# Graph network with two layers on one core: layer 0's bias moved from a matmul to GpSimd, and two comparisons joined

## The reference, cut to what matters

```
h = relu(layernorm(x))
deg = segment_sum(ones, src); feat = h * clip(deg, 1)**-0.5
s = relu(segment_sum(feat[src], dst))
x = x + (s @ W.T + b)                       # layer 0
h = relu(layernorm(x))
m = segment_sum(h[src] @ W_msg.T + b_msg + edge_embed[type], dst)
x = x + gru(m, h, W_ih, W_hh, b_ih, b_hh)   # layer 1
```

## Time and profile before

| | before |
|---|---|
| median of 3 executions | 918.85 us (918.78 to 919.85) |
| the profiled execution | 920.79 us, of which the span is 918.8 us |
| granted TensorE clock over the span | 0.984 |
| TensorE, VectorE, ScalarE, GpSimd busy | 845.8, 772.6, 502.3, 96.9 us |

### The profile page before, as it was taken

How to read it: one execution, slowest core, us unless ns; L and a number is a source line. 1 busy time by engine, 2 the same in 40 slices (tenths; PEclk the granted TensorE clock), 3 DMA queues, 4 the chain that set the end, 5 groups by cost and what they waited for, 6 DMA issues and landing times.

```text
span 918.8 us, 21032 instructions
## 1 busy us (share of the span) xinstructions
PE 845.8 (92%) x8962; PEld 755.5 (82%) x8962; DVE 772.6 (84%) x1044; ACT 502.3 (55%) x924; POOL 96.9 (11%) x77
## 2 busy tenths in 40 slices
PE   2353899999999999999999999999999999999996
PEld 2242788889888888988889988989889888988985
DVE  5898999999999999999999991568766766766876
ACT  1579588888888888888888884211111111111011
POOL 6880203003020030100000000000000000000000
PEclk9995899999999999999999999999999999999998
DMA  3642434336444344543335510497667667667750
GB/s 89 136 142 74 166 145 168 153 151 236 195 179 167 152 172 195 211 181 147 152 146 212 211 34 13 156 299 267 236 272 283 226 248 299 236 233 290 260 211 20
DMA packets 38332, 169.17 MB, mean 184 GB/s; under 512 B 8132, under 2 KB 21387, under 8 KB 35288
## 3 DMA queue, kind: packets, MB, share of 16 engines
q1 hardware_dynamic: 31898, 159.98, 46.2%
q0 software_dynamic: 6000, 6.48, 2.9%
q10 hardware_dynamic: 334, 1.29, 0.5%
HBM read 87.67 MB, written 79.74 MB: 182 GB/s over the span
## 4 chain that ended last, share of the span: by engine, by line
PE 52%; DVE 31%; issue 6%; ACT 5%; POOL 4%; DMA 1%; SPq 0%; DVEq 0%; POOLq 0%; ACTq 0%
PE ps L1323 29%; DVE work L743 11%; DVE work L736 11%; PE ps L1182 9%; PE ps L1171 5%; DVE work L751 4%; POOL tab L494 3%; ACT ring L976 2%; ACT tab L987 1%; PE ps L1275 1%; PE ps L1278 1%; PE ps L1280 1%; PE ps L1276 1%; PE ps L1277 1%; PE ps L1279 1%
## 5 line engine op out<-in xcount | busy, mean ns | idle before, releaser
L1171 PE MATMUL ps<-work 128*128 128x106 f16 x3125 | 431.3, 216 | 46.7 <-ACT ring L976 29.0
L1182 PE MATMUL ps<-ring,tab 125*128 125x250 f16 x2500 | 417.2, 272 | 0.7 <-ACT ring L981 0.7
L976 ACT ACTIVATE ring<-ps 128x848 f16<-128x848 f32 x375 | 330.6, 884 | 75.3 <-PE ps L1171 68.8
L1171 PEld LDWEIGHTS ps<-work 128*128 128x128 f16 x3125 | 286.5, 101 | 70.5 <-ACT ring L976 33.2
L1323 PE MATMUL ps<-ring,tab 125*128 125x250 f16 (+1 forms) x2500 | 277.0, 269 | 0.0
L1323 PEld LDWEIGHTS ps<-ring,tab 125*128 125x128 f16 (+1 forms) x2500 | 242.4, 97 | 28.7
L1182 PEld LDWEIGHTS ps<-ring,tab 125*128 125x128 f16 x2500 | 244.5, 98 | 25.3 <-ACT ring L981 0.9
L736 DVE TENSOR_TENSOR work<-iota_row,mch 128x3906 f16<-128x3906 f16 x100 | 223.4, 2234 | 1.0 <-PE ps L1171 0.5
L743 DVE TENSOR_TENSOR work<-iota_w,mch 128x1550 f16<-128x1550 f16 x200 | 188.1, 981 | 0.0
L824 DVE TENSOR_TENSOR work<-work,ring 125x3250 f16<-125x3250 f16 (+1 forms) x92 | 161.6, 1780 | 0.0
L1119 ACT ACTIVATE tab<-ps,bg 128x250 f32<-128x250 f32 x25 | 11.8, 471 | 147.7 <-PE ps L1276 146.9
(11 more groups left out here) (187 smaller groups left out, 617.3 us busy)
## 6 DMA issues: line engine op xcount, KB each, us to landing
adjacency<-ring SPq DMA_DIRECT2D x23, 2937.5 KB
ring<-adjacency SPq DMA_DIRECT2D x46, 812.5 KB, 6.4
ring<-adjacency SPq DMA_DIRECT2D x46, 750.0 KB, 9.0
adjacency<-ring SPq DMA_DIRECT2D x23, 183.1 KB
out<-x_sb SPq DMA_DIRECT2D x24, 125.0 KB
h_turned<-hst SPq DMA_DIRECT2D x23, 125.0 KB, 2.0
tab<-h_turned SPq DMA_DIRECT2D x23, 125.0 KB, 2.0
x_sb<-x SPq DMA_DIRECT2D x3, 560.0 KB
```

What stands on the lines that cost most here:

```text
L976: act.activation(to(x * 2 * u, 2, x), ps[:, s:s + 2, 0:x * SLOTS].rearrange("p b (x h) -> p h b x", h=SLOTS), ACT.Copy).then_inc(sem("evac ...
L1171: last = pe.matmul(ps[:, 2 * (u % 2) + i // BANKW, o:o + WCOLS], lohot[:, s, k, :], combo[:, s, k, :], start=True, stop=True)
L1182: mm = pe.matmul(psD[c % 2], tabv[0][P, h, s, :], adj[c % 2][P, h, :], start=i == 0, stop=i == 2 * BLOCKS - 1)
```

## The change

It has three parts. `split_bias`, its tiles and the bias matmul leave; `psX` holds the product alone. GpSimd adds the bias to x itself, both nodes of a chunk in one instruction of 256 elements, 25 of them; they stand in its queue behind the gather of chunk 11 and a wait for the finished table (`tab0`), since the table is made of x without the bias, and ahead of the gather of chunk 12. `post0_x_vector` waits for its chunk's addition (`biased`). And in `onehots` one comparison covers the columns of both nodes, where two did.

```
--- before.py
+++ after.py
@@ -69,7 +69,7 @@
 
 SEMAPHORES = """
 heads_in weights_in dst_in x_in0 x_in1 x_in2 x_in3 x_in4 ends_set ends_in
-iotas consts consts0 headhots hist totals counted rows_i bias_parts later_in cand_in0 cand_in1 cand_in2 cand_in3 cand_in4 cand_in5 run_i
+iotas consts consts0 headhots hist totals counted rows_i biased later_in cand_in0 cand_in1 cand_in2 cand_in3 cand_in4 cand_in5 run_i
 runs_in0 runs_in1 runs_in2 runs_in3 runs_in4 runs_in5
 squares sq_sum wm_norm gsc_set scaled g_col emb_in odd0 odd1 a_square a_root scale0 h0 rows_v tab0_hi tab0
 fields lo_keys turned mch_keys mch onehot built spent evac adj_out0 adj_out1 types_moved
@@ -183,8 +183,6 @@
         ones = sb("ones", [128, 128], F32)
         onesh = sb("onesh", [128, 1], F16)
         iota_s = sb("iota_s", [128, CHUNKS + 1], F16)
-        onesb = sb("onesb", [128, LO], BF16)
-        b_parts = sb("b_parts", [128, CB, D], BF16)
         thr = sb("thr", [128, CHUNKS], F32)
         thr_odd = sb("thr_odd", [128, CHUNKS], F32)
         thr_key = sb("thr_key", [128, CHUNKS], F32)
@@ -249,8 +247,6 @@
         sq, at = carve(early, at, 3, D)
 
         embf = temps[0:TYPES, :].bitcast(F32)[:, 0:D]
-        bias_high, at = carve(early, at, D)
-        bias_rest, at = carve(early, at, D)
         cand, at = carve(early.bitcast(I32), at, CHUNKS, CAND)
         signs, at = carve(early, at, JUNK * CAND // 2)
         signs = signs.bitcast(F16).rearrange("p (k n) -> p k n", k=JUNK)
@@ -476,9 +472,7 @@
             gp.tensor_scalar(ident3[:, :], ident[:, :], float(TB), None, ALU.mult)
             gp.tensor_scalar(nident3[:, :], ident[:, :], -float(TB), None, ALU.mult)
             gp.iota(beyond[:, :], [[WIN, AHEAD]], base=KEY + WIN, channel_multiplier=0, allow_small_or_imprecise_dtypes=True)
-            gp.memset(onesb[:, :], 1.0)
             gp.memset(least[:, :], 2e-35)
-            gp.memset(b_parts[:, :, :], 0.0)
             gp.iota(thr_key[:, :], [[WIN, CHUNKS]], base=-KEY, channel_multiplier=BLOCKS,
                     allow_small_or_imprecise_dtypes=True)
             gp.iota(iota_row[:, :], [[1, LO + 1]], base=KEY, channel_multiplier=0, allow_small_or_imprecise_dtypes=True)
@@ -509,7 +503,16 @@
             run_edges(2)
             for m in (3, 4, 5):
                 candidates(m)
-            for g in range(3, CHUNKS):
+            for g in range(3, 3 + RAW):
+                run_edges(g)
+            for g in range(3 + RAW, 6 + RAW):
+                run_edges(g)
+
+            gp.wait_ge(sem("tab0"), TBATCHES)
+            for k in range(CHUNKS):
+                gp.tensor_tensor(x_sb[P, blocks(k), :], x_sb[P, blocks(k), :],
+                                 b0_sb[P, :].unsqueeze(1).broadcast_to([LO, CB, D]), ALU.add).then_inc(sem("biased"), 1)
+            for g in range(6 + RAW, CHUNKS):
                 run_edges(g)
 
 
@@ -599,7 +602,6 @@
             v.memset(epst[:, :], EPS)
             search_heads(v, ch)
             weight_squares(v, ch)
-            split_bias(v, ch)
             v.wait_ge(sem("consts"), 1)
             search_runs(v, ch, 0)
             row_stats(v, ch, 0, 0, XB)
@@ -607,23 +609,6 @@
             row_stats(v, ch, 1, 0, XB)
             unpack(v, ch, 0, 1)
             scale_weights(v, ch)
-
-        def split_bias(v, ch):
-
-            ch.did(v.tensor_copy(b_parts[0:1, 0, :], b0_sb[0:1, :]))
-            ch.did(v.tensor_copy(bias_high.bitcast(BF16)[:, 0:D], b0_sb[:, :]))
-            ch.wait()
-            ch.did(v.tensor_copy(b_parts[0:1, 1, :], b_parts[0:1, 0, :]))
-            ch.did(v.tensor_tensor(bias_rest, b0_sb[:, :], bias_high.bitcast(BF16)[:, 0:D], ALU.subtract))
-            ch.wait()
-            ch.did(v.tensor_copy(bias_high.bitcast(BF16)[:, D:2 * D], bias_rest))
-            ch.wait()
-            ch.did(v.tensor_tensor(bias_rest, bias_rest, bias_high.bitcast(BF16)[:, D:2 * D], ALU.subtract))
-            ch.did(v.tensor_copy(b_parts[32:33, :, :], bias_high.bitcast(BF16)[32:33, D:2 * D].unsqueeze(1)
-                                 .broadcast_to([1, CB, D])))
-            ch.wait()
-            v.tensor_copy(b_parts[64:65, :, :], bias_rest[64:65, :].unsqueeze(1).broadcast_to([1, CB, D]))\
-             .then_inc(sem("bias_parts"), 1)
 
         def weight_squares(v, ch):
 
@@ -738,14 +723,12 @@
                 iota_row[:, 0:even].rearrange("p (n t) -> p n t", t=2).unsqueeze(1)
                     .broadcast_to([128, n, even // 2, 2]),
                 lo2.unsqueeze(2).broadcast_to([128, n, even // 2, 2]), ALU.is_equal))
-            for d in range(WIN):
-                cols = slice(SLOTS * d, SLOTS * d + BLOCKS)
-                ch.did(v.tensor_tensor(
-                    combo[:, s, 0:n, cols].rearrange("p k (a t) -> p k a t", t=2),
-                    iota_w[:, cols].rearrange("p (n t) -> p n t", t=2).unsqueeze(1)
-                        .broadcast_to([128, n, BLOCKS // 2, 2]),
-                    col2.unsqueeze(2).broadcast_to([128, n, BLOCKS // 2, 2]), ALU.is_equal))
-            ch.wait(but=WIN)
+            blocks_of = lambda a: a.rearrange("p k (d h) -> p k d h", d=WIN)[:, :, :, 0:BLOCKS]
+
+            ch.did(v.tensor_tensor(blocks_of(combo[:, s, 0:n, :]),
+                                   blocks_of(iota_w[:, :].unsqueeze(1).broadcast_to([128, n, WCOLS])),
+                                   col2.unsqueeze(2).broadcast_to([128, n, BLOCKS, 2]), ALU.is_equal))
+            ch.wait(but=1)
             if b == 0:
                 v.wait_ge(sem("mch"), c + 1)
             v.tensor_tensor(typehot[:, s, 0:n, :, :],
@@ -755,6 +738,7 @@
 
         def post0_x_vector(v, ch, k):
 
+            v.wait_ge(sem("biased"), k + 1)
             v.wait_ge(sem("psX"), k + 1)
             v.tensor_tensor(x_sb[P, blocks(k), :], psX, x_sb[P, blocks(k), :], ALU.add).then_inc(sem("x1"), 1)
             v.wait_ge(sem("x1"), k + 1)
@@ -1189,12 +1173,9 @@
             positive(pe, sem("tab_lo"), k)
             if k == 0:
                 pe.wait_ge(sem("later_in"), 16)
-                pe.wait_ge(sem("bias_parts"), 1)
             for j in range(CB):
-                pe.matmul(psX[:, j, :], aggr[:, LO * j:LO * (j + 1)], w0_sb[:, :], start=j == 0, stop=False,
-                          skip_group_check=True)
-            pe.matmul(psX, onesb[0:65, :], b_parts[0:65, :, :], start=False, stop=True, skip_group_check=True)\
-              .then_inc(sem("psX"), 1)
+                last = pe.matmul(psX[:, j, :], aggr[:, LO * j:LO * (j + 1)], w0_sb[:, :], start=True, stop=True)
+            last.then_inc(sem("psX"), 1)
 
         def post0_turn_tensor(pe, k):
             pe.wait_ge(sem("h1"), k + 1)
```

22 lines of the change are left out of this document (1 added, 21 removed).

## The result

| | before | after |
|---|---|---|
| median of 5 executions | 918.85 us (918.78 to 919.85) | 924.21 us (923.82 to 924.46) |
| the profiled execution, its span | 920.79, 918.8 us | 924.46, 922.7 us |
| granted TensorE clock over the span | 0.984 | 0.975 |

The changed kernel is slower by 5.4 us: the ratio to before is 1.0053, with a 95% interval of 1.0042 to 1.0064. The forecast was 922.8 us with a range of 914 to 930, and slower as its likeliest side.

A forecast was written before the change was run, and what follows sets the result against it. VectorE and TensorE were taken as a nearly level pair, VectorE slower by 0.56 us per three chunks. The terms -1.4 - 2.8 - 2.4 + 10.5 gave +3.9 us on 918.85, so 922.8 us, range 914.0 to 930.0.

The forecast's parts named there:

- The additions: GpSimd's 25 additions, in chunks 2 to 4: each costs VectorE 0.46 us by its SBUF reads, 11.5 us together.
- The lower bound of 0.08 us: VectorE's loss per addition if the addition's length does not matter: 2.0 us for all 25.
- the upper one of 0.77 us: VectorE's loss per addition if GpSimd keeps it out for reads and writes, 768 elements: 19.2 us for all 25.
- The joined comparison: VectorE's two comparisons of 1550 elements become one of 3100: 0.08 us saved per batch, 0.32 per chunk.
- The rival of a slow form: The joined comparison falls to one element per cycle, 150 us more, some 1070 us; chance 0.03.
- The start: GpSimd's gathers up to 60 us: without its two memsets and VectorE's bias split, -1.4 us, from -0.4 to -2.
- The stalls: TensorE's five 0.56 us stalls in chunks 5 to 17 go as both engines stand level: -2.8 us.
- The lower bound, -1 where VectorE still trails: The smaller gain from TensorE's stalls in chunks 5 to 17 if VectorE still trails: -1 us.
- The matmul: The bias matmul leaves TensorE's path, 0.11 us per chunk over 20 chunks and 2 at the tail: -2.4 us.
- The rule weighed in the prediction: Second to issue at SBUF blocks fully until the first finishes: additions would cost 14 us, the whole change +6.4.

The follow-up runs named there:

- wide_adds: The changed kernel with the bias sum made in five GpSimd instructions (one of 256 elements, four of 1536) instead of 25: 927.16 us, ratio 1.0085.
- sets: The changed kernel with each addition replaced by a memset of 256 elements of a spare tile, each waiting for the one before: 915.36 us, one execution.
- join_alone: The kernel before with only the comparison joined: 918.31 us, ratio 0.9984.
- no_adds: The changed kernel without GpSimd's 25 additions and the waits for them, layer 0's bias left out of the result: 915.21 us, ratio 0.9953.
- after_keys: The changed kernel with ScalarE's row keys at unit 10 instead of unit 7 of every third chunk: 924.07 us, ratio 1.0052.
- bias_alone: The changed kernel with the two comparisons of before in place of the joined one: 935.25 us, ratio 1.0170.
- early_adds: The changed kernel with the additions moved up, five at a time once their table rows are computed, ahead of chunks 9 to 11's gathers: 919.48 us, ratio 1.0004.
- spaced_adds: The changed kernel with the two comparisons of before, each addition waiting for the semaphore of the one before it: 929.27 us, ratio 1.0109.

## Why the prediction was right, and which of its numbers were not

**The additions: right mechanism, 0.42 us each where the sum took 0.46, and the size in part by luck.** Forecast for 25 were 11.5 us; VectorE's chunks 2 to 4 show 10.6: 22 turns of 0.35 to 0.55 us, and three additions that slipped in free. The 1 ns per value behind the 0.46 was read from a wrong row. The 0.26 us belongs to a CAST of 128 elements, L475; the scalings behind it, L476 and L477, are not "the same work": by themselves they take 0.50 us from start to start (join_alone, below). That wide_adds gave 1.05 ns per value for an addition confirms the figure, and not the way to it. The lower bound of 0.08 us (length does not matter) is excluded by wide_adds, the upper one of 0.77 us (reads and writes both count) by sets.

**The joined comparison: 0.08 us per batch forecast, 0.068 measured.** The rival of a slow form fell.

**The start: -1.4 us forecast, 2.5 between the two profiled executions, some 0.7 in the medians.** The forecast was 0.4 for the memsets and 1.0 for GpSimd's wait for `run_i`. join_alone keeps both the memsets and the split, and its GpSimd shows this:

```profile
3.29 0.52 POOL L476 TENSOR_SCALAR ident<-ident 128x128 f16<-128x128 f32 x1
3.79 0.53 POOL L477 TENSOR_SCALAR nident<-ident 128x128 f16<-128x128 f32 x1
...
15.16 1.21 POOL L501 DMA_INDIRECT raw<-edges,run_i  x1 [0.40 <-DVE run_i L559]
```

The wait is 0.40 us with the split in place, not 1.28, and the two scalings take 0.52 and 0.53 us, not 0.77 and 1.04. The same gather in the change, where the two scalings take 0.52 and 0.53 us too:

```profile
14.72 1.21 POOL L495 DMA_INDIRECT raw<-edges,run_i  x1 [0.35 <-DVE run_i L562]
```

The gather of chunk 0 starts 2.18 us earlier than in the earlier trace rows, but only 0.44 us earlier than in join_alone. Part of the gain that I read off was a mark of the execution that had been profiled. VectorE's first comparison with two inputs started at 3.18 us there, and GpSimd had to wait for it twice; in join_alone and in the change it started at 3.42 and 3.40, and GpSimd didn't wait. In keys_alone, which keeps the split too, VectorE's started at 3.17, the scalings took 0.77 and 1.04 us again, and the gather of chunk 0 starts at 16.13 after a wait of 0.60. Of the three kernels with the split in place, chunk 2 begins at 97.93 us in join_alone, 98.26 in keys_alone and 99.33 before; in the change, no_adds and after_keys, without it, at 96.84, 96.78 and 97.55. By the medians no_adds lies 3.1 us under join_alone, of which 2.4 are the matmul, so some 0.7 is left for the start. The prediction itself noted that the profiled execution was 1.9 us above the median, and should have asked where; 1.1 to 1.4 of it stand at the beginning of chunk 2, and the rest I have not traced. That is most of why the medians differ by 5.4 us and the profiled executions by 3.9.

**The stalls: -2.8 us forecast, -1.0 measured, the step that failed most.** The five third chunks keep 0.41, 0.41, 0.33, 0.31 and 0.33 us of 0.56. The step is "Both engines then stand level, and the five stalls of chunks 5 to 17 go". Level is not enough: each of them alone is held up by something. One is ScalarE's row keys, which I had not priced; the other is VectorE, once TensorE is faster too. The lower bound, -1 where VectorE still trails, was the right end.

**The matmul: -2.4 us forecast,** 0.11 us per chunk measured (19.49 to 19.38), so right.

**The sum in medians.** All but the additions: forecast -7.6 (the joined comparison's -1.0 in chunks 2 to 4 included), measured -4.1 (no_adds, good to some 1.2 us). join_alone tells where: comparison and stalls brought 1.0 us instead of 3.8, and what is left, start and matmul, 3.1 instead of 3.8. The additions: forecast 11.5, measured 9.0. Both gain and loss were too large, by 3.5 and by 2.5 us, and so the total of +3.9 stands beside a measured +4.9 against the before of that set and +5.4 against the first. The side and the mechanism were earned; the closeness was luck.

**The rule weighed in the prediction.** The Trainium skill (SBUF — State Buffer, Who interferes with whom) says that the second to issue blocks fully until the first finishes. In bias_alone the trace agrees and goes beyond it: one VectorE instruction was blocked through 25 GpSimd instructions. In the change it agrees less: VectorE lost 0.55 us at most to additions that take 0.68 us from start to start. The Trainium skill's figure (GPSIMD Engine Reference, Performance versus the Vector engine) gave 0.56 us as an estimate for one addition; the train shows 0.68.

**The better kernel.** keys_alone, the kernel before with the joined comparison and the row keys at unit 10, took 916.28 us and is the fastest that computes all of the reference: 0.9962 (0.9949 to 0.9976) of before. Only the kernel without the additions is faster (no_adds, 915.21), but the bias must be added somewhere, and no place that is free was found.

## What to carry to other kernels

Work moved to an idle GpSimd is not free when VectorE is on the path: in this kernel an addition cost VectorE about 1 ns for each value that GpSimd read from SBUF, a copy less, and that belongs on VectorE's time. Put such work where VectorE idles: early_adds paid the same 10.5 us, and 5.1 of it were hidden. When two engines are nearly level, a gain on one is worth only the distance to the next bound, and that bound can be a third engine's small piece, here ScalarE's row keys. And when the profiled execution is above the median, find out which of its rows are its own before a term of the sum is read from them.

## What the runs showed of the hardware that was not expected

- GpSimd can keep VectorE out for a whole row of instructions. Twenty-five additions of 256 elements without a wait between them ran in 17.05 us, and one VectorE comparison stood still through all of them (bias_alone). With the same additions and the joined comparison they took turns, 40.18 us. What decides between the two was not found; a semaphore wait between the additions brought the turns back (spaced_adds).
- It goes the other way too: in early_adds one addition of GpSimd's was held for 6.13 us while VectorE's instructions followed one another.
- VectorE pays for GpSimd instructions that read: mostly 0.51 to 0.55 us for 2 x 256 values, 3.22 us for 2 x 1536, 0.17 to 0.20 us for 1 x 256, nothing for a memset of 256.
- The cost falls on the VectorE instruction that GpSimd gets ahead of, and does not go by that one's length: +0.5 us on one of 279 elements as on one of 3100. It fell on instructions that read one tile as well: the 20 of L703 took 9.42 us in place of 5.18 beside ten additions (early_adds).
- At the start, the same two GpSimd instructions took 0.52 and 0.53 us in 12 of the 14 profiled kernels and 0.77 and 1.04 us in two (before, keys_alone), where VectorE's first comparison had started 0.2 us earlier.
